# A four-layer graph network on one core: row sums of the adjacency moved to ScalarE, a lighter VectorE, and another order of the first steps

## The chip, the cores and the metric

One core of a Trainium2 chip runs the whole program. The metric is the device time of one execution in microseconds (us). The kernel before took 1369.27 us, the median of 3 runs (1369.18 to 1369.64). Measurements of this kernel tell a difference of about 0.2% (2.7 us) from none.

## The reference, cut to what matters

`x` is 4096x128, `adj` is 4096x4096, both float32. Four layers follow one another; each normalises its input, rectifies it, multiplies it by `adj`, and adds the layer's result to `x`:

```python
h = jnp.maximum(_layernorm(x, axis=-1), 0.0)
x = x + _L0_gnn_ref(h, adj, L0_gnn_W, L0_gnn_b)      # relu([h, adj @ h] @ W.T + b)
h = jnp.maximum(_layernorm(x, axis=-1), 0.0)
x = x + _L1_gnn_ref(h, adj, L1_gnn_W, L1_gnn_b)      # needs the row sums of adj
h = jnp.maximum(_layernorm(x, axis=-1), 0.0)
x = x + _L2_gnn_ref(h, adj, ...)                     # adj @ h, then a GRU cell
h = jnp.maximum(_layernorm(x, axis=-1), 0.0)
x = x + _L3_gnn_ref(h, adj, ...)                     # row sums, top 4 neighbours of every row by distance, adj again
```

Layers 1 and 3 scale by the inverse root of the row sums of `adj` (layer 1 with 1 added), so the sums of all 4096 rows have to be known before layer 1's operand is ready.

## The kernel before, in words

**Tiling.** The rows are cut into 8 row blocks of 512 (`NB`, `BLK`). A pass over `adj` multiplies each of the 8 row blocks with 8 column blocks. The unit of work is a *visit*: 2 tiles of 128 columns by 512 rows of the transposed `adj` (`at_in`, 512 KB), so that a row block of a pass has 16 visits (`UNITS`). Each visit's unit is loaded by SP into one of 10 slots of `ring` (L391), and the load of visit n waits until TensorE has used visit n-10 (`used`) and, in the first pass, until VectorE has summed it (`summed`). Layers 0 to 3 are passes 0 to 3, a fourth sparse-plus-dense product (pass 4) ends the program, and between passes 3 and 4 lies a search for the 4 nearest rows.

**Two ways to multiply.** A *whole* visit feeds the float32 tile directly (L469, two matmuls, which the trace shows as 4 records). A *split* visit has ScalarE round the unit to `A_hi` (`upper`, L803 to L810, recorded at L679), VectorE subtract to get `A_lo` (`lower`, L1111), and TensorE run three faster matmuls per tile (L464 to L466). Passes 1 to 3 split every visit. In pass 0 a visit is split if it serves two layers at once (a *shared* visit, `feeds` of two) or if the planner thinks VectorE has time. Six `A_hi` slots (`STAGED`) let ScalarE run up to six split visits ahead of TensorE.

**The plan.** Class `Plan` (L74) walks the visits with an estimated clock `self.us` (1.38 us for a split feed, 1.73 us for a whole one) and a second one for VectorE, `self.vector_us`. In pass 0 it adds 1.22 us for each unit that VectorE adds up and, if the clock leaves room, splits the visit and adds another 1.22 us (L172 to L174). It also places the small steps of each finished row block (`CHAIN`, L41) after certain visits, in the order in which each engine issues them; an engine never goes past a step that waits.

**Row sums.** `add_unit` (L985) adds every unit of pass 0 to `colsum` on VectorE, `fold` (L999) closes a row block, `degree_sums` (L548) lets TensorE sum over the partitions, and `degrees` (L1010) copies the result out; `degree_roots` (L743) follows on ScalarE. Then `residual`, `roots` and `normalise` on VectorE and ScalarE, `h_transposes` (L505) on TensorE, `rectify` (L717) on ScalarE, and `operand` (L530) on TensorE make the next layer's operand of this row block.

**The start.** For each row block b of `x` VectorE takes `statistics` (L949) and `normalise` (L958), TensorE transposes the result (`first_transposes`, L511), ScalarE rectifies it (`first_rectify`, L838), TensorE multiplies by the neighbour weight (`first_operand`, L520), and ScalarE copies that out to `G_first` (`first_operand_out`, L842). TensorE does the transposes of row blocks 0 and 1, then the product of row block 0, then the first visit (L611 to L615); the rest of the row blocks follow every second visit. ScalarE's loop over b is at L849.

Of the kernel before, what the change touches and what calls it, by code (L numbers as in the profile page):

```python
# [5 lines left out]
P = 128  # L6
N = 4096
BLK = 512
TPB = BLK // P
# [29 lines left out]
VECTOR_US, VECTOR_ROWS_US, BEHIND_US = 1.22, 6.0, 0.0  # L39
LEAD = {"PE": 0, "ACT": 4, "DVE": 3}  # L40
# [33 lines left out]
class Plan:  # L74
# [29 lines left out]


# [47 lines left out]

    def next_of(self, p, b, left):
# [7 lines left out]
    def visit(self, p, b, kb, left, may_share):  # L162
# [65 lines left out]
def gnn_stack(nc, x_in, at_in, pack_in, scaled_rows, out):  # L228
# [4 lines left out]
    with ctx:  # L233
# [47 lines left out]
        sq_aug = at("sq_aug", [P, NB, BLK], r32, sums_at)  # L281
        gate_r, new, gate_z, cand = (colsum[:, i, :] for i in range(4))
# [8 lines left out]
        rstd = sb("rstd", [P, TPB])  # L291
        degree = sb("degree", [P, NB, TPB])
        deg_pair = sb("deg_pair", [P, 2, TPB])
# [32 lines left out]
        used, summed = sem("used"), sem("summed")  # L326
# [3 lines left out]
        nat_full = sem("nat_full")  # L330
        stats_ready, std_ready, hn_ready = sem("stats_ready"), sem("std_ready"), sem("hn_ready")
# [30 lines left out]
        row_end = lambda p, b: PLAN.spans[p, b, p][1] + 1  # L362
        slot_of = lambda v: PLAN.split_count[v.n] % STAGED
# [17 lines left out]
        def _(sp):  # L381
# [3 lines left out]
            def load_unit(v):  # L385
                s = v.n % SLOTS
                if v.n >= SLOTS:
                    sp.wait_ge(used, v.n - SLOTS + 1)
                    if v.n - SLOTS < NB * UNITS:
                        sp.wait_ge(summed, v.n - SLOTS + 1)  # L390
# [23 lines left out]
        def _(pe):  # L414
# [262 lines left out]
        def _(act):  # L677
# [133 lines left out]

            def step(name, p, b):
# [24 lines left out]

            def first_rectify(b):  # L838
# [106 lines left out]
        def _(dve):  # L945
# [39 lines left out]
            def add_unit(v):  # L985

                s, j = v.n % SLOTS, v.n % UNITS
# [6 lines left out]
                else:  # L994
                    dve.wait_ge(summed, v.n - 1)
# [3 lines left out]
            def fold(b):  # L999

                dve.wait_ge(summed, UNITS * (b + 1))
# [8 lines left out]
            def degrees(b):  # L1010
# [3 lines left out]
                v_.tensor_copy(degree[:, b, :], ps[:, AUX, 0:TPB])  # L1014
                v_.tensor_copy(deg_pair[:, 0, :], ps[:, AUX, 0:TPB])
# [328 lines left out]
```

## Time and profile before

| what | value |
|---|---|
| median of 3 runs | 1369.27 us |
| the profiled execution | 1368.41 us |
| its span, first to last instruction | 1366.5 us |
| TensorE busy | 1313.5 us (96%) |
| VectorE busy | 1129.6 us (83%) |
| ScalarE busy | 795.4 us (58%) |
| GpSimd busy | 134.2 us (10%) |
| bytes moved | 291.49 MB, mean 213 GB/s |
| granted TensorE clock, mean | 0.996 |

The busy times are averages over stages with different limits. Matmul records overlap, so the time of a visit is read from starts, not from durations. Pass 0 lies between 14 us and 323 us; passes 1 to 3 reach to about 900 us, the search to about 1156 us, the last pass to the end.

### The profile page before, as it was taken

The numbers are of one execution on the slowest core, as the hardware profiler recorded it, in microseconds if no ns is written. First come the engines' busy times: TensorE is split into PE (matmuls) and PEld (weight loads), VectorE is DVE, ScalarE is ACT, GpSimd is POOL, SyncE is SP. The second block draws the span as 40 slices with busy tenths as digits, with TensorE's granted clock in tenths as the row PEclk, the third lists the DMA queues.
The fourth block names the chain that finished last, engine by engine and source line by source line (L and its number), as shares of the span: only waits on it lengthen the run. The fifth ranks groups of instructions, "written<-read, shape, count | busy, mean of one in ns | idle before, by whom it ended". The sixth has DMA issues, their size and how long they took to land.

```text
span 1366.5 us, 15557 instructions
## 1 busy us (share of the span) xinstructions
PE 1313.5 (96%) x5452; PEld 960.5 (70%) x5452; DVE 1129.6 (83%) x1538; ACT 795.4 (58%) x1173; POOL 134.2 (10%) x146
## 2 busy tenths in 40 slices
PE   7999999999899999999999999998999999999997
PEld 4556677778777875778777777876677777656664
DVE  8998889988999797767664898769999999845665
ACT  2322233446666587766555678655666565568885
POOL 0000000000000000000000100000000000077775
PEclk9999999999999999999999999999999999999999
DMA  9777766557876695566555889910111111499996
GB/s 354 232 261 243 233 203 209 190 185 244 298 265 227 192 352 170 192 225 204 190 186 172 306 285 321 350 58 1 39 54 54 54 39 54 156 354 385 383 383 231
DMA packets 82862, 291.49 MB, mean 213 GB/s; under 512 B 10849, under 2 KB 10977, under 8 KB 82785
## 3 DMA queue, kind: packets, MB, share of 16 engines
q1 hardware_dynamic: 78048, 280.01, 59.5%
q0 software_dynamic: 4736, 10.49, 2.3%
q8 instruction: 44, 0.72, 0.2%
q14 instruction: 34, 0.27, 0.1%
HBM read 286.27 MB, written 4.19 MB: 213 GB/s over the span
## 4 chain that ended last, share of the span: by engine, by line
PE 66%; DVE 29%; ACT 2%; issue 2%; DMA 0%; SPq 0%; ACTq 0%; DVEq 0%
PE ps L469 15%; PE ps L464 14%; PE ps L466 14%; PE ps L465 13%; DVE best_at L1187 9%; DVE rows_T L1183 9%; DVE A_lo L1111 5%; PE ps L539 1%; PE ps L567 1%; PE ps L568 1%; PE ps L502 1%; PE ps L508 1%; DVE hn L966 1%; PE ps L526 1%; DVE stats L951 1%
## 5 line engine op out<-in xcount | busy, mean ns | idle before, releaser
L679 ACT ACTIVATE A_hi<-ring 128x1024 fp32r<-128x1024 f32 x378 | 390.3, 1055 | 104.5 <-PE ps L466 91.9
L1111 DVE TENSOR_TENSOR A_lo<-ring,A_hi 128x1024 fp32r<-128x1024 f32 x333 | 395.7, 1218 | 55.3 <-ACT A_hi L679 53.0
L464 PE MATMUL ps<-A_hi,G_odd_hi 128*128 128x512 f32 x602 | 256.2, 426 | 2.1 <-DVE A_lo L1111 2.1
L466 PE MATMUL ps<-A_hi,G_odd_lo 128*128 128x512 f32 x602 | 235.9, 392 | 0.0
L465 PE MATMUL ps<-A_lo,G_odd_hi 128*128 128x512 f32 x602 | 234.8, 390 | 0.0
L679 ACT ACTIVATE scores<-ps,neg_sq 128x1024 f32<-128x1024 f32 x128 | 137.4, 1112 | 51.6 <-PE ps L640 33.8
L464 PE MATMUL ps<-A_hi,G_even_hi 128*128 128x512 f32 x386 | 162.7, 421 | 0.2 <-DVE A_lo L1111 0.2
L469 PE MATMUL ps<-ring,G_last 128*128 128x512 f32 x332 | 152.5, 592 | 0.0
L466 PE MATMUL ps<-A_hi,G_even_lo 128*128 128x512 f32 x386 | 150.7, 391 | 0.0
L465 PE MATMUL ps<-A_lo,G_even_hi 128*128 128x512 f32 x386 | 150.3, 389 | 0.0
L1183 DVE MAX8 rows_T<-scores 128x8 f32<-128x4096 f32 x32 | 141.3, 4415 | 7.3 <-ACT scores L679 7.3
L1187 DVE FIND_INDEX8 best_at<-rows_T,scores 128x8 uint32<-128x4096 f32 x32 | 141.4, 4419 | 0.0
L464 PEld LDWEIGHTS ps<-A_hi,G_odd_hi 128*128 128x128 f32 x602 | 113.5, 188 | 34.3 <-issue 13.0
L465 PEld LDWEIGHTS ps<-A_lo,G_odd_hi 128*128 128x128 f32 x602 | 113.6, 189 | 30.5 <-issue 9.6
L996 DVE TENSOR_TENSOR colsum<-colsum,ring 128x1024 f32<-128x1024 f32 x112 | 133.6, 1218 | 0.0
L466 PEld LDWEIGHTS ps<-A_hi,G_odd_lo 128*128 128x128 f32 x602 | 113.2, 188 | 24.9
L1305 POOL DMA_INDIRECT landing<-scaled_rows,best_at x128 | 123.7, 967 | 43.9 <-issue 36.0
L637 PE MATMUL ps<-sq_aug,ones 128*128 128x512 f32 x256 | 108.8, 425 | 14.8 <-ACT scores L679 14.1
L469 PE MATMUL ps<-ring,G_first 128*128 128x512 f32 x252 | 113.3, 592 | 0.0
L640 PE MATMUL ps<-z_hi,z_lo 128*128 128x512 f32 x256 | 101.7, 397 | 0.0
L638 PE MATMUL ps<-z_hi 128*128 128x512 f32 x256 | 101.5, 396 | 0.0
L469 PEld LDWEIGHTS ps<-ring,G_last 128*128 128x128 f32 x332 | 62.7, 189 | 55.0 <-issue 49.9
(136 smaller groups left out, 1516.1 us busy)
## 6 DMA issues: line engine op xcount, KB each, us to landing
ring<-adj_t SPq DMA_DIRECT2D x524, 512.0 KB, 4.8
X<-x_rows SPq DMA_DIRECT2D x8, 256.0 KB, 7.0
scaled_rows<-G_last POOLq DMA_DIRECT2D x8, 256.0 KB, 2.7
landing<-scaled_rows,best_at POOLq DMA_INDIRECT x128, 5.4
out_rows<-X SPq DMA_DIRECT2D x8, 256.0 KB, 5.7
pack<-packed SPq DMA_DIRECT2D x1, 836.0 KB, 14.7
pack<-packed SPq DMA_DIRECT2D x1, 192.0 KB, 3.5
```

The source lines that it names most:

```text
L464: mm(acc, G_hi[odd][:, kb, t, :], hi, start=start, stop=False)
L465: mm(acc, G_hi[odd][:, kb, t, :], lo, start=False, stop=False)
L466: done = mm(acc, G_lo[odd][:, kb, t, :], hi, start=False, stop=stop)
L469: done = mm(acc, G[:, kb, t, :], ring[:, s, k, :], start=start, stop=stop)
L637: mm(ps[:, bank, :], ones2[:, :], sq_aug[:, c, :], start=True, stop=False)
L640: last = mm(ps[:, bank, :], lo, z_hi[:, c, :], start=False, stop=True)
L679: return nc.scalar.activation(out_ap, in_ap, func, **k)
L996: ins = v_.tensor_tensor(half, half, ring[:, s, :, :], ALU.add)
L1111: v_.tensor_tensor(A_lo[:, s, :, :], ring[:, s, :, :], hi, ALU.subtract).then_inc(lower_ready, 1)
L1183: own.add(v_.max(best[:, seek[i], :], scores[i % 2][:, :]))
L1187: v_.max_index(best_at[:, seek[i], :], best[:, seek[i], :], scores[i % 2][:, :]).then_inc(scanned, 1)
L1305: pool.indirect_dma_start(out=landing[:, k, r, :], out_offset=None, in_=scaled_rows, in_offset=bass.IndirectOffsetOnAxis(ap=best_at[:, t, ...
```

## The change

1. TensorE's start: after the transposes of row block 0 comes its weight product (`first_operand(0)`), then the first visit; the transposes of row block 1 stand behind the first visit, the product of row block 1 and the transposes of row block 2 behind the second.
2. From row block 1 on ScalarE normalises `x` (`first_normalise`): VectorE makes a scale and a shift per row (`first_scales`), ScalarE applies them in four activations per row block, between `first_rectify(b)` and `first_operand_out(b)`.
3. A second copy of `adj`, in row order, is passed in (`rows_in`). Quarters of 1024 columns of some row blocks (`ROW_PIECES`) are no longer added up on VectorE: one quarter of row blocks 2 and 6, two quarters of 3, 4 and 5. Instead GpSimd loads 32 pieces of 128x1024 (512 KB each) into two buffers, the load of piece i after piece i-2 is summed, and ScalarE adds each up with the accumulator of a copy (`add_piece`). That takes 32 of 128 `add_unit` calls away. `degrees` adds the parts.
4. The planner's VectorE clock no longer counts the missing units. With the same rule it splits 21 more visits of pass 0: 3 in row block 2, 5 in row block 3, 6 in row block 4, 4 in row block 5 and 3 in row block 6. All other visits, their order and the plan from visit 112 on are the same; a few steps of row blocks 1 to 5 stand one visit later.
5. SP's loads wait for `summed` only where VectorE adds the unit.

```diff
+PIECE = 1024
+ROW_PIECES = ((), (), (2,), (2, 3), (2, 3), (2, 3), (3,), ())
...
+    def by_columns(self, b, u):
+        return u * UK * P // PIECE not in ROW_PIECES[b]
...
-                self.vector_us = max(self.vector_us, self.us - 4 * VECTOR_US) + VECTOR_US
+                self.vector_us = max(self.vector_us, self.us - 4 * VECTOR_US)
+                self.vector_us += self.by_columns(b, kb * HALVES + half) * VECTOR_US
                 split = split or b > 0 and self.vector_us + VECTOR_US <= self.us + SPLIT_US + BEHIND_US
...
             first_transposes(0)
-            first_transposes(1)
             first_operand(0)
             for v in PLAN.visits[:UNITS]:
                 visit(v)
-                if v.u % HALVES == 0 and v.u // HALVES + 1 < NB:
+                if v.u == 0:
+                    first_transposes(1)
+                elif v.u == 1:
+                    first_operand(1)
+                    first_transposes(2)
+                elif v.u % HALVES == 0 and v.u // HALVES + 1 < NB:
...
+            def add_piece(b, n, c):
+
+                i = pieces.index((b, n, c))
+                act.wait_ge(row_loaded[i % 2], 16 * (i // 2 + 1))
+                f(row_piece[:, i % 2, :], row_piece[:, i % 2, :], ACT.Copy,
+                  accum_out=row_sum[:, b, n, c:c + 1]).then_inc(row_summed, 1)
...
+            def first_normalise(b):
+                act.wait_ge(scale_ready, b)
+                if b >= 2:
+                    act.wait_ge(hT_full, b - 1)
+                for n in range(TPB):
+                    last = f(first_hn[b % 2][:, n, :], X[:, b, n, :], ACT.Identity,
+                             scale=first_scale[:, b % 2, n:n + 1], bias=first_shift[:, b % 2, n:n + 1])
+                last.then_inc(hn_ready, 1)
...
                 first_rectify(b)
+                if b + 1 < NB:
+                    first_normalise(b + 1)
                 first_operand_out(b)
...
                 if v.split:
                     upper(v)
+                if v.n in PLAN.row_sums:
+                    add_piece(*PLAN.row_sums[v.n])
                 for name, p, b in PLAN.due["ACT"].get(v.n, ()):
...
-                v_.tensor_copy(degree[:, b, :], ps[:, AUX, 0:TPB])
-                v_.tensor_copy(deg_pair[:, 0, :], ps[:, AUX, 0:TPB])
-                v_.tensor_scalar(deg_pair[:, 1, :], ps[:, AUX, 0:TPB], 1.0, None, ALU.add).then_inc(pair_ready, 1)
+                if not ROW_PIECES[b]:
+                    own.add(v_.tensor_copy(degree[:, b, :], ps[:, AUX, 0:TPB]))
+                else:
+                    dve.wait_ge(row_summed, 1 + max(i for i in range(len(pieces)) if pieces[i][0] == b))
+                    own.add(v_.tensor_tensor(degree[:, b, :], row_sum[:, b, :, 0], ps[:, AUX, 0:TPB], ALU.add))
...
+            for i, (b, n, c) in enumerate(pieces):
+                if i < 2:
+                    pool.wait_ge(used, b * UNITS - SLOTS)
+                else:
+                    pool.wait_ge(row_summed, i - 1)
+                pool.dma_start(row_piece[:, i % 2, :], rows_in[b, n, ROW_PIECES[b][c], :, :]).then_inc(row_loaded[i % 2], 16)
```

**TensorE at the start of the program.** `hn` and `nat` hold the normalised rows of even and odd row blocks, `in_a` the rectified ones. Before:

```order
L516 MATMUL ps<-pack,hn 128x128 x4
L516 MATMUL ps<-pack,nat 128x128 x4
L526 MATMUL ps<-pack,in_a 128x128 x4
L430 MATMUL ps<-in_a,pack 128x512
L469 MATMUL ps<-ring,G_first 128x512 x2
L516 MATMUL ps<-pack,hn 128x128 x4
L526 MATMUL ps<-pack,in_a 128x128 x4
```

With the change:

```order
L542 MATMUL ps<-pack,hn 128x128 x4
L552 MATMUL ps<-pack,in_a 128x128 x4
L456 MATMUL ps<-in_a,pack 128x512
L495 MATMUL ps<-ring,G_first 128x512 x2
L542 MATMUL ps<-pack,nat 128x128 x4
L495 MATMUL ps<-ring,G_first 128x512 x2
L552 MATMUL ps<-pack,in_a 128x128 x4
L542 MATMUL ps<-pack,hn 128x128 x4
L495 MATMUL ps<-ring,G_first 128x512 x2
```

The four transposes of row block 1 have moved from the second place to behind the first visit, and the third visit now stands directly behind the product of row block 1 and the transposes of row block 2.

**ScalarE at the seam between row blocks 2 and 3.** `rows_T` is row block 2's result being moved out, `deg_root`, `std` and `hTs` are `degree_roots`, `roots` and `rectify` of row block 2, `A_hi` is one split visit, `row_piece` one piece of row sums. Before:

```order
L679 ACTIVATE rows_T<-ps,pack 128x512 [waits nat_full,used]
L679 ACTIVATE A_hi_65<-ring_58 128x1024 [waits used,at_loaded3]
L679 ACTIVATE deg_root<-deg_pair 128x8 [waits pair_ready]
L679 ACTIVATE std<-meanvar,eps_ln 128x4 [waits stats_ready]
L679 ACTIVATE A_hi_65<-ring_58 128x1024 [waits used,at_loaded6]
L679 ACTIVATE hTs<-ps 128x512 [waits g_full,hT_full]
```

With the change:

```order
L709 ACTIVATE rows_T<-ps,pack 128x512 [waits nat_full,used]
L709 ACTIVATE A_hi_65<-ring_58 128x1024 [waits used,at_loaded3]
L709 ACTIVATE row_piece_68,row_sum<-row_piece_68 128x1024 [waits row_loaded0]
L709 ACTIVATE deg_root<-deg_pair 128x8 [waits pair_ready]
L709 ACTIVATE A_hi_65<-ring_58 128x1024 [waits used,at_loaded4]
L709 ACTIVATE std<-meanvar,eps_ln 128x4 [waits stats_ready]
L709 ACTIVATE A_hi_65<-ring_58 128x1024 [waits used,at_loaded5]
L709 ACTIVATE row_piece_68,row_sum<-row_piece_68 128x1024 [waits row_loaded1]
L709 ACTIVATE A_hi_65<-ring_58 128x1024 [waits used,at_loaded6]
L709 ACTIVATE A_hi_65<-ring_58 128x1024 [waits used,at_loaded7]
L709 ACTIVATE row_piece_68,row_sum<-row_piece_68 128x1024 [waits row_loaded0]
L709 ACTIVATE hTs<-ps 128x512 [waits g_full,hT_full]
```

Between `std` and `hTs` there was one `A_hi`; now there are three and two pieces.

## Rows read from the trace of the kernel before

**Rows 1.** The chain that ended last, by engine.

```profile
PE 66%; DVE 29%; ACT 2%; issue 2%; DMA 0%; SPq 0%; ACTq 0%; DVEq 0%
```

**Rows 2.** Waits of TensorE, 14 to 330 us: engine, line, cause: total us, times, longest.

```profile
PE ps L508 <- DVE hn L966: 1.1, 1, 1.1
PE ps L539 <- ACT hTs L679: 0.7, 1, 0.7
```

**Rows 3.** Chain in order of time (start, us, what) and TensorE's timeline, by visits.

```profile
22.27 3.44 PE ps L469 x8
27.04 3.44 PE ps L469 x8
...
88.00 6.87 PE ps L469 x16
```

**Rows 4.** TensorE's timeline inside row block 7, one feed apart.

```profile
299.90 0.39 PE L464 MATMUL ps<-A_hi,G_odd_hi 128*128 128x512 f32 x1
...
301.26 0.39 PE L464 MATMUL ps<-A_hi,G_even_hi 128*128 128x512 f32 x1
```

**Rows 5.** Timeline of the start: start, us, engine, line, operation, [idle before].

```profile
6.68 1.08 PE L516 MATMUL ps<-pack,hn 128*128 128x128 f32 x4 [6.68 <-DVE hn L966]
...
7.96 0.58 ACT L679 ACTIVATE in_a<-ps 128x512 f32<-128x512 f32 x1
...
10.68 1.12 PE L516 MATMUL ps<-pack,nat 128*128 128x128 f32 x4 [2.92 <-DVE nat L966]
...
11.59 1.92 PE L526 MATMUL ps<-pack,in_a 128*128 128x128 f32 x8
...
14.26 1.91 PE L469 MATMUL ps<-ring,G_first 128*128 128x512 f32 x4
```

**Rows 6.** Groups of ScalarE and VectorE instructions by form: xcount, busy us, mean ns.

```profile
L679 ACT ACTIVATE A_hi<-ring 128x1024 fp32r<-128x1024 f32 x378 | 390.3, 1055 | 104.5 <-PE ps L466 91.9 <-DMA ring<-adj_t 11.5
L1111 DVE TENSOR_TENSOR A_lo<-ring,A_hi 128x1024 fp32r<-128x1024 f32 x333 | 395.7, 1218 | 55.3 <-ACT A_hi L679 53.0
L679 ACT ACTIVATE in_a<-ps 128x512 f32<-128x512 f32 x24 | 14.3, 594 | 87.8 <-PE ps L466 78.9 <-PE ps L508 8.8
L679 ACT ACTIVATE rows_T<-ps,pack 128x512 f32<-128x512 f32 x8 | 5.5, 683 | 0.5 <-PE ps L469 0.5
L679 ACT ACTIVATION_READ_ACCUMULATOR hn<-nat 128x1 f32 x32 | 6.1, 190 | 0.0
```

**Rows 7.** Timeline at the seam of row blocks 2 and 3, three engines.

```profile
118.28 1.02 PE L430 MATMUL ps<-in_a,pack 128*128 128x512 f32 x2
...
129.01 0.60 PE L508 MATMUL ps<-pack,hn 128*128 128x128 f32 x4
...
119.55 1.06 ACT L679 ACTIVATE A_hi<-ring 128x1024 fp32r<-128x1024 f32 x1
...
126.42 0.30 ACT L679 ACTIVATE std<-meanvar,eps_ln 128x4 f32<-128x4 f32 x1 [4.04 <-DVE meanvar L955]
...
131.92 1.14 ACT L679 ACTIVATE G_odd_hi<-ps,inv_root 128x128 fp32r<-128x128 f32 x4 [1.68 <-PE ps L539]
...
126.97 1.12 DVE L966 TENSOR_SCALAR hn<-X,meanvar,rstd 128x128 f32<-128x128 f32 x4
```

**Rows 8.** Stretches (us), busy us (records) of each engine, granted clock, DMA share, GB/s.

```profile
118.28:154.62 36.34, 36.34 (x143) 24.79 (x142) 32.41 (x49) 10.99 (x17) 0.00 (x0) 1.00 0.71 232
154.62:193.30 38.68, 38.68 (x157) 27.41 (x156) 34.23 (x50) 12.17 (x18) 0.00 (x0) 1.00 0.68 217
1230.00:1330.00 100.00, 100.00 (x333) 60.98 (x333) 63.32 (x102) 86.45 (x147) 75.93 (x80) 1.00 1.02 383
```

**Rows 9.** Loads into `ring`, 1160 to 1366 us: issue to landing.

```profile
DMA to landing us min/median/max: 3.4/6.0/7.1
```

**Rows 10.** GpSimd's gathers: durations ns min/median/max, first and last start.

```profile
L1305 POOL DMA_INDIRECT landing<-scaled_rows,best_at x128: 940/944/1411, 1194.8 to 1356.3; - x128
```

**Rows 11.** Waits of VectorE, 60 to 330 us.

```profile
DVE A_lo L1111 <- ACT A_hi L679: 6.1, 4, 2.5
```

More of the change, by code:

```diff
@@ L102, in __init__ @@
         self.place(0.0, flush=True)
+        self.sum_count, self.row_sums, n = {}, {}, 0
+        for v in self.visits[:NB * UNITS]:
+            self.sum_count[v.n], n = n, n + self.by_columns(v.b, v.u)
+        self.sum_count[NB * UNITS] = n
+        for b in range(NB):
+            parts = [(b, n, c) for n in range(TPB) for c in range(len(ROW_PIECES[b]))]
+            for i, part in enumerate(parts):
+                self.row_sums[b * UNITS + (2 * i + 1) * UNITS // (2 * len(parts))] = part
         ended = [b * HALVES + half for b in sorted(range(NB), key=lambda b: self.rank[3, b]) for half in range(HALVES)]
@@ L325, in gnn_stack @@
         at_loaded = [sem(f"at_loaded{s}") for s in range(SLOTS)]
-        used, summed = sem("used"), sem("summed")
+        used, summed, row_summed = sem("used"), sem("summed"), sem("row_summed")
+        row_loaded = [sem(f"row_loaded{i}") for i in range(2)]
         upper_ready, lower_ready = sem("upper_ready"), sem("lower_ready")
@@ L362, in gnn_stack @@
         row_end = lambda p, b: PLAN.spans[p, b, p][1] + 1
+        pieces = [(b, n, c) for b in range(NB) for n in range(TPB) for c in range(len(ROW_PIECES[b]))]
         slot_of = lambda v: PLAN.split_count[v.n] % STAGED
@@ L388, in load_unit @@
                     sp.wait_ge(used, v.n - SLOTS + 1)
-                    if v.n - SLOTS < NB * UNITS:
-                        sp.wait_ge(summed, v.n - SLOTS + 1)
+                    before = PLAN.visits[v.n - SLOTS]
+                    if before.n < NB * UNITS and PLAN.by_columns(before.b, before.u):
+                        sp.wait_ge(summed, PLAN.sum_count[before.n] + 1)
                 sp.dma_start(ring[:, s, :, :], at_in[v.b, v.u, :, :, :]).then_inc(at_loaded[s], 16)
@@ L994, in add_unit @@
                 else:
-                    dve.wait_ge(summed, v.n - 1)
+                    dve.wait_ge(summed, n - 1)
                     ins = v_.tensor_tensor(half, half, ring[:, s, :, :], ALU.add)
@@ L1138, in step, with first_scales, first_statistics @@
                     square_parts(b)
+            def first_scales(b):
+                dve.wait_ge(std_ready, b + 1)
+                if b >= 3:
+                    dve.wait_ge(hn_ready, b - 1)
+                own.add(v_.reciprocal(first_scale[:, b % 2, :], std[:, b % 2, :]))
+                own.settle()
+                v_.scalar_tensor_tensor(first_shift[:, b % 2, :], meanvar[:, b % 2, :, 0], -1.0, first_scale[:, b % 2, :],
+                                        ALU.mult, ALU.mult).then_inc(scale_ready, 1)
+            def first_statistics(b):
+                dve.wait_ge(x_loaded[b], 16)
+                statistics(b, b, b % 2)
             def first_rows(b):
                 if b + 1 < NB:
-                    dve.wait_ge(x_loaded[b + 1], 16)
-                    statistics(b + 1, b + 1, (b + 1) % 2)
-                normalise(b, b, b % 2, first_hn[b % 2], 2)
-            dve.wait_ge(x_loaded[0], 16)
-            statistics(0, 0)
+                    first_statistics(b + 1)
+                first_scales(b)
+            first_statistics(0)
             normalise(0, 0, 0, first_hn[0], 2)
-            dve.wait_ge(x_loaded[1], 16)
-            statistics(1, 1, 1)
-            first_rows(1)
+            first_statistics(1)
+            first_scales(1)
+            first_statistics(2)
             for v in PLAN.visits[:UNITS]:
@@ L1168, in _ @@
             for v in PLAN.visits[UNITS:PLAN.rows_end]:
-                if v.feeds[0] == 0:
+                if v.feeds[0] == 0 and PLAN.by_columns(v.b, v.u):
                     add_unit(v)
@@ L1324 @@
     at = np.ascontiguousarray(get("adj").reshape(NB, BLK, UNITS, UK, P).transpose(0, 2, 4, 3, 1))
+    rows = np.ascontiguousarray(get("adj").reshape(NB, TPB, P, N // PIECE, PIECE).transpose(0, 1, 3, 2, 4))
     w0, w1, wm = get("L0_gnn_W"), get("L1_gnn_W"), get("L2_gnn_W_msg")
```

20 lines of the change are left out of this document (16 added, 4 removed).

## The prediction

> **What bounds the kernel now.** I read the chain of waits first: TensorE holds 66% of it and VectorE 29% [rows 1]. In order of time TensorE holds it from 14 us to 323 us, the whole of pass 0; VectorE takes over in passes 1 and 2 and in the search. The change touches pass 0 and the start only, so I then read who TensorE waits for there: two waits in 316 us, 1.1 us for `normalise` of row block 0 and 0.7 us for a `rectify` [rows 2]. Pass 0 is TensorE's own work and little else: what makes its work shorter makes the program shorter, and every new wait costs its full length.
>
> What a visit costs is read from starts. Sixteen records of whole visits, four visits, hold the chain for 6.87 us [rows 3]: 1.72 us each. The six matmuls of a split feed start 301.26 - 299.90 = 1.36 us apart from the next six [rows 4]. A split visit that serves one layer is 0.36 us cheaper on TensorE, if ScalarE and VectorE have prepared it in time.
>
> **The sum, edit by edit.**
>
> *More split visits.* 21 visits of pass 0 change from whole to split: 21 x 0.36 = **-7.5 us**. It is the main term.
>
> Their cover: each needs one `A_hi` on ScalarE (1.055 us) and one `A_lo` on VectorE (1.22 us) [rows 6]. VectorE gives up 32 `add_unit` calls and takes 21 subtractions of the same size, 11 fewer over the pass, about 13 us of work. In row block 4, the tightest, it goes from 9 + 16 = 25 such instructions to 15 + 8 = 23 while TensorE's time falls by 6 x 0.36 = 2.2 us. From 34.2 us busy in 38.7 us [rows 8] it comes to 31.8 in 36.5. VectorE stays ahead: cost nothing, and if it were behind, the rival on pass 1 below says what that costs.
>
> *Rows of `adj` summed on ScalarE.* One piece is like an `A_hi` plus the reading of the accumulator, 190 ns that partly overlap [rows 6]: between 1.06 and 1.25, I take 1.15 us. Eight pieces and five more `A_hi` bring row block 3 from 11.0 us busy [rows 8] to 25.5 us in a stage of 34.5. The mean is harmless; the order is not. ScalarE's waits are where the steps stand, and everything queues behind them. I follow the seam of row blocks 2 and 3, counting from 118.28 [rows 7].
>
> TensorE: `h_transposes` started at +10.7; two of the four visits between the seam's steps and it become split, so now at +10.0. One split visit and 0.35 us of transposes later, at +11.7, it wants `operand`, which needs `rectify`. ScalarE: `A_hi` starts at +1.3 [rows 7] and ends at +2.3, piece +3.5, `degree_roots` +4.3 (VectorE's sums are ready at about +4.1), `A_hi` +5.3. `std` stood at +8.1, after one `add_unit` that has gone, so it comes about 1 us sooner and ends at +7.5. Then three `A_hi` and two pieces, 3 x 1.05 + 2 x 1.15 = 5.4 us: +12.9. `rectify` takes 0.6 [rows 6]: +13.5. TensorE waits **+1.8 us**, once. `hn` itself was ready at +9.8 [rows 7] for +10.7 and is ready at +8.9 for +10.0.
>
> The same count at the seam after row block 3 (steps one visit later, so only two `A_hi` and one piece lie between) gives +11.9 for a need at +12.5: nothing. After row blocks 4 and 5 a sum and a subtraction now stand ahead of `normalise`, which ends at about +10.5 for a need at +10.7: I put **+0.3 us** for both. After row block 5 `operand` moves one visit behind `h_transposes`, with which it shared a visit; that takes out the 0.7 us wait of [rows 2]: **-0.7 us**. `degrees` grows by up to two tiny instructions with waits between, about 0.3 us, inside these margins; the 1.1 us wait of row block 0 stays.
>
> *The loads.* A unit or a piece is 0.524 MB; at the highest rate of the trace, 383 GB/s with the DMA engines full [rows 8], that is 1.37 us. Row block 3 moves 16 + 8 = 24 of them: 32.9 us in a stage of 34.5; row block 4 the same in 36.5. It fits, with 5% to spare, and ten slots of `ring` smooth it: no cost. The Trainium skill (DMA: Bandwidth & Descriptors, "Where 436 GB/s comes from") puts what HBM gives one core at about 358 GB/s. By that rule row block 3 would need 35.1 us and lose up to 0.6 us; the trace's 383 stands against it here.
>
> A piece's landing has to be quick too, for ScalarE waits for it in order. Two buffers mean that piece i is asked for when i-2 is summed, four visits ahead: at least 5.4 us in split visits of one feed, 10.9 in shared ones. Loads in the fullest stretch land after 3.4 to 7.1 us, median 6.0 [rows 9], and a GpSimd issue takes 0.94 us [rows 10]. So early in row blocks 3 to 5 a piece may be 1 to 2 us late, against ScalarE's lead of up to six split visits. I put nothing.
>
> *The start.* `rectify` of row block 0 ends at 7.96 + 0.58 = 8.54 [rows 5]. The weight product waited for the second transposes and began at 11.59; from there to the first visit, at 14.26, were 2.67 us, partly at half pace: four transposes take 1.08 us at 6.68 and 1.12 at 10.68 [rows 5], but 0.60 at 129.01 [rows 7]. Now it begins at about 8.6. At the old pace the first visit starts at 11.3; all at half pace nearer 12.1. I take 11.7: 2.5 us earlier.
>
> From this goes what the new order costs. The transposes of row block 1 (0.35 us) now lie behind the first visit. ScalarE's normalising of a row block is four activations like 1.14 us for four of the same size [rows 7], plus a per-row operand more, 0.683 - 0.594 = 0.09 us each [rows 6]: 1.5 us. In the second row block it stands ahead of `first_operand_out`, so the third visit waits about 0.3 us; the transposes of row block 3 wait for rectify and normalise behind that, 0.7 us. Later the cycle of 4.77 us [rows 3] leaves ScalarE 3.44 us for 3.0 us of work between product and transposes: no wait. The start gives 2.5 - 0.35 - 0.3 - 0.7 = **-1.2 us**, bounds -2.2 and -0.3. The seven normalisings that VectorE is rid of lie beside TensorE and bring nothing, as the split operands at the end of row block 0 are gated by its last product.
>
> *After pass 0.* From visit 112 on all is the same. VectorE waits 6.1 us for `A_hi` in pass 0 [rows 11], mostly at its end: it carries no debt into pass 1, so pass 1 starts earlier by what pass 0 gained, and the rest slides.
>
> Sum: -7.5 + 1.8 + 0.3 - 0.7 - 1.2 = **-7.3 us**. The profiled execution took 1368.41 us, 1.9 us more than its span, and comes to 1361.1; the median of the runs shown is 0.86 us above it. Predicted: **1362.0 us**, 0.5% faster.
>
> **Rivals.**
>
> *No queue on ScalarE.* If `rectify` is in time at the seam (pieces nearer 1.06 us, the seam's steps earlier), the 1.8 and 0.3 us go: 1359.9 us. For it: everything hangs on a 1.8 us overhang of an order counted. Chance 0.17.
>
> *Pieces land late, a little.* If issue to landing is 8 us with contention, two pieces take 9.2 us against 5.4 us early in each of row blocks 3 to 5; four such pairs of buffers eat ScalarE's lead and leave about 1.5 us per block: 1366.5 us. For it: the DMA engines are 95% taken. Against: loads at 383 GB/s still land in 6.0 us. Chance 0.13.
>
> *Pass 1 swallows it.* If VectorE, not TensorE's end of pass 0, sets when pass 1 proceeds, or the added splits are not ready in time, the 7.5 us is gone: 1369.3 less 1.2 plus 1 is 1369 us. For it: VectorE holds the chain right behind 323 us. Against: the 6.1 us that it waits just before [rows 11]. Chance 0.09.
>
> *Slower: pieces starve ScalarE.* Eight pieces in a row block go through two buffers, so the block lasts at least 4 x (issue + landing + 1.15). In row block 3 that exceeds 34.5 us from 7.5 us on, in row block 4 from 8.0, in row block 5 from 8.7. At 9 us the blocks last 40.6 us, 6.1 + 4.1 + 1.4 = 11.6 us more, and the total is 1373.6 us; it decides above about 8.6 us. What could make it so is GpSimd's issue being held up beside a VectorE that is busy nine tenths of the time. Against: with VectorE at 63% [rows 8] the gathers took 944 ns, 1411 at most [rows 10], where the blocks need 2 us more on every piece. The Trainium skill (SBUF: State Buffer, "SBUF: two separate sides") says that a DMA issued from GpSimd cannot get its descriptors written while VectorE runs a fast float32 copy; by that rule the two `colsum` copies that open a row block would hold up a piece. Chance 0.06.
>
> **How the numbers follow.** Forecast 0.55 (own range 1360 to 1365), no queue 0.17, late pieces 0.13, pass 1 swallows it 0.09, starving 0.06. The range reaches down past the no-queue case with the better start (1359) and up past the late pieces to 1367.5; it leaves out the last two cases and the tails. Faster by over 0.2% is below 1366.5: 0.55 + 0.17 + half of 0.13 and little else, 0.8. Within 0.2%: 0.13. Slower: 0.07. About 0.2% is what measurement tells from nothing.
>
> **What would show it.** In the changed profile: the first visit at 11.7 us; L508's counterpart waiting about 1 us in row block 1 and `operand` waiting 1.8 us behind `rectify` in row block 3 and nowhere else; starts of `begin`'s product 33 us apart in row block 2, 36 in row block 3, 36.5 in row block 4; pieces of about 1.15 us with landings of 5 to 7 us; DMA share near full in row block 3. I am wrong if TensorE waits for `A_lo` in row blocks 3 to 5 (late pieces or ScalarE's queue), or if pass 0 ends 7 us earlier and the later stages do not.

## The result, and the profile after

The changed kernel takes 1361.59 us, the median of 5 runs (1361.28 to 1362.47), against 1369.27 (5 runs beside them): ratio 0.9938, 95% interval 0.9927 to 0.9949. The forecast was 1362.0. The profiled execution took 1361.59 us, with a span of 1359.8 us against 1366.5.

The chain and the waits of TensorE up to 330 us in the profile after, to be laid beside [rows 1, 2]:

```profile
PE 66%; DVE 30%; ACT 3%; issue 2%; DMA 0%; ACTq 0%; DVEq 0%
```

```profile
PE ps L534 <- DVE hn L1016: 1.2, 1, 1.2
PE ps L565 <- ACT hTs L709: 0.8, 1, 0.8
PE ps L542 <- ACT nat L709: 0.3, 1, 0.3
PE ps L495 <- ACT G_first L709: 0.2, 1, 0.2
```

The bound is what it was. The wait of 1.1 us for `hn` in row block 1 is still there (1.2). The 0.7 us wait for `hTs` has gone from row block 6 and one of 0.8 us has come in row block 3. The last two are new, at the start.

Where pass 0 is shortened can be read from where each row block starts: `begin`'s product, L430 before and L456 after, on TensorE. The timeline of the kernel after:

```profile
50.13 1.02 PE L456 MATMUL ps<-in_a,pack 128*128 128x512 f32 x2
...
83.53 1.02 PE L456 MATMUL ps<-in_a,pack 128*128 128x512 f32 x2
...
116.84 1.02 PE L456 MATMUL ps<-in_a,pack 128*128 128x512 f32 x2
...
152.53 1.02 PE L456 MATMUL ps<-in_a,pack 128*128 128x512 f32 x2
...
189.10 1.02 PE L456 MATMUL ps<-in_a,pack 128*128 128x512 f32 x2
...
228.37 1.02 PE L456 MATMUL ps<-in_a,pack 128*128 128x512 f32 x2
...
270.35 1.02 PE L456 MATMUL ps<-in_a,pack 128*128 128x512 f32 x2
...
316.78 0.95 PE L582 MATMUL ps<-ones,nat 128*128 128x1 f32 x8
```

| row block | starts before, us | starts after, us | lasts before | lasts after | splits added |
|---|---|---|---|---|---|
| 1 | 50.65 | 50.13 | 33.33 | 33.40 | 0 |
| 2 | 83.98 | 83.53 | 34.30 | 33.31 | 3 |
| 3 | 118.28 | 116.84 | 36.34 | 35.69 | 5 |
| 4 | 154.62 | 152.53 | 38.68 | 36.57 | 6 |
| 5 | 193.30 | 189.10 | 40.69 | 39.27 | 4 |
| 6 | 233.99 | 228.37 | 43.97 | 41.98 | 3 |
| 7 | 277.96 | 270.35 | 46.43 | 46.43 | 0 |

(Row block 7 is counted to the `degree_sums` that close it, 324.39 and 316.78 us.) Pass 0 ends 7.6 us earlier, of which 0.5 comes from before row block 1. The shift is 7.7 us still at the first `lap_rows` step of pass 3 (782.3 to 774.6 us), 6.9 us at the second (790.7 to 783.8) and when the search starts (902.0 to 895.1) and 6.7 us at the end of the span.

Stretches of row blocks 3 and 4 after, against [rows 8] (columns as there):

```profile
116.84:152.53 35.69, 34.84 (x153) 26.54 (x152) 29.26 (x44) 24.87 (x38) 3.70 (x7) 1.00 0.95 346
152.53:189.10 36.57, 36.57 (x170) 29.61 (x168) 32.92 (x49) 27.83 (x43) 4.88 (x9) 1.00 0.95 358
```

ScalarE goes from 11.0 to 24.9 us busy in row block 3 and from 12.2 to 27.8 in row block 4, the DMA share from 0.7 to 0.95. VectorE goes from 32.4 to 29.3 and from 34.2 to 32.9. TensorE stays busy but for 0.85 us. The pieces:

```profile
L1363 POOL DMA_DIRECT2D row_piece<-adj_rows x32: 528/528/963, 64.6 to 233.0; - x32
L709 ACT ACTIVATE row_piece<-row_piece x32: 1039/1057/1079, 69.3 to 252.5; 128x1024 f32<-128x1024 f32 x32
L709 ACT ACTIVATION_READ_ACCUMULATOR row_piece<-row_piece x32: 180/187/218, 70.2 to 253.5; 128x1 f32 x32
...
DMA to landing us min/median/max: 4.0/6.6/8.1
```

The issue costs 0.53 us (the gathers of [rows 10] take 0.94), the landing 6.6 us in the median. ScalarE waited for pieces 8 times, 11.8 us in all, and TensorE never noticed.

The seam of row blocks 2 and 3, ScalarE's timeline after (start, us, instruction):

```profile
118.11 1.06 ACT L709 ACTIVATE A_hi<-ring 128x1024 fp32r<-128x1024 f32 x1
119.05 1.06 ACT L709 ACTIVATE row_piece<-row_piece 128x1024 f32<-128x1024 f32 x1
...
123.98 0.30 ACT L709 ACTIVATE std<-meanvar,eps_ln 128x4 f32<-128x4 f32 x1 [1.96 <-DVE meanvar L1005]
124.19 1.04 ACT L709 ACTIVATE A_hi<-ring 128x1024 fp32r<-128x1024 f32 x1
125.14 1.05 ACT L709 ACTIVATE row_piece<-row_piece 128x1024 f32<-128x1024 f32 x1
...
126.17 1.99 ACT L709 ACTIVATE A_hi<-ring 128x1024 fp32r<-128x1024 f32 x2
128.07 1.04 ACT L709 ACTIVATE row_piece<-row_piece 128x1024 f32<-128x1024 f32 x1
...
129.11 0.57 ACT L709 ACTIVATE hTs<-ps 128x512 f32<-128x512 f32 x1
```

and what TensorE does with it:

```profile
129.74 1.16 PE L565 MATMUL ps<-pack,hTs 128*128 128x128 f32 x8 [0.85 <-ACT hTs L709]
```

`std` ends at +7.4 us from the row block's start, `hTs` at +12.8, the product starts at +12.9. TensorE was ready for it at +12.05 (0.85 us of waiting). It is the queue that the prediction counted, ending 0.7 us sooner than the +13.5 counted there.

### The profile page after: what moved, and what is told of

Its sections match the earlier page's. It is cut to its first block, busy times and chain, and to the rows that moved or that the text cites. A ratio compares the mean times of both kernels' runs of the same rounds, so it can differ in the third digit from the quotient of the medians.

```text
span 1359.8 us, 15719 instructions
## 1 busy us (share of the span) xinstructions
PE 1309.5 (96%) x5494; PEld 969.0 (71%) x5494; DVE 1112.4 (82%) x1509; ACT 861.1 (63%) x1286; POOL 151.5 (11%) x178
## 4 chain that ended last, share of the span: by engine, by line
PE 66%; DVE 30%; ACT 3%; issue 2%; DMA 0%; ACTq 0%; DVEq 0%
PE ps L490 14%; PE ps L492 14%; PE ps L491 14%; PE ps L495 12%; DVE best_at L1258 9%; DVE rows_T L1254 9%; DVE A_lo L1170 5%; PE ps L565 1%; PE ps L593 1%; PE ps L594 1%; PE ps L528 1%; DVE hn L1016 1%; DVE stats L1001 1%; PE ps L534 1%; PE ps L552 1%
## 5 line engine op out<-in xcount | busy, mean ns | idle before, releaser
L709 ACT ACTIVATE A_hi<-ring 128x1024 fp32r<-128x1024 f32 x399 | 412.6, 1055 | 113.1 <-PE ps L492 89.6
L1170 DVE TENSOR_TENSOR A_lo<-ring,A_hi 128x1024 fp32r<-128x1024 f32 x354 | 420.2, 1218 | 68.6 <-ACT A_hi L709 66.1
L490 PE MATMUL ps<-A_hi,G_even_hi 128*128 128x512 f32 x428 | 178.8, 418 | 0.2 <-DVE A_lo L1170 0.2
L492 PE MATMUL ps<-A_hi,G_even_lo 128*128 128x512 f32 x428 | 167.1, 390 | 0.0
L491 PE MATMUL ps<-A_lo,G_even_hi 128*128 128x512 f32 x428 | 166.7, 390 | 0.0
L667 PE MATMUL ps<-sq_aug,ones 128*128 128x512 f32 x256 | 108.6, 424 | 13.6 <-ACT scores L709 12.9
L669 PE MATMUL ps<-z_lo,z_hi 128*128 128x512 f32 x256 | 102.0, 398 | 0.0
L1047 DVE TENSOR_TENSOR colsum<-colsum,ring 128x1024 f32<-128x1024 f32 x80 | 95.8, 1217 | 0.0
```

Source lines behind the costliest of these rows:

```text
L490: mm(acc, G_hi[odd][:, kb, t, :], hi, start=start, stop=False)
L491: mm(acc, G_hi[odd][:, kb, t, :], lo, start=False, stop=False)
L492: done = mm(acc, G_lo[odd][:, kb, t, :], hi, start=False, stop=stop)
L667: mm(ps[:, bank, :], ones2[:, :], sq_aug[:, c, :], start=True, stop=False)
L669: mm(ps[:, bank, :], hi, z_lo[:, c, :], start=False, stop=False)
L709: return nc.scalar.activation(out_ap, in_ap, func, **k)
```

## The experiments

The theory that goes into them: the gain is 21 x 0.36 us of cheaper TensorE work, VectorE's relief is only what makes it possible, one wait behind the pieces takes some back, and the start brings little.

### Parts of the change alone

**The start's order alone**, on the kernel before:

```diff
             first_transposes(0)
-            first_transposes(1)
             first_operand(0)
             for v in PLAN.visits[:UNITS]:
                 visit(v)
-                if v.u % HALVES == 0 and v.u // HALVES + 1 < NB:
+                if v.u == 0:
+                    first_transposes(1)
+                elif v.u == 1:
+                    first_operand(1)
+                    first_transposes(2)
+                elif v.u % HALVES == 0 and v.u // HALVES + 1 < NB:
```

> The kernel before with TensorE's new order at the start and nothing else: VectorE still normalises all of x, no pieces, no added splits. My theory: the first visit starts about 2 us earlier (near 12.3 us), 0.35 us is lost to the transposes that now lie behind it, and VectorE, which is as busy as TensorE in the first row block (4.9 us of work per cycle of 4.77), gives back up to 0.7 us: 0.9 us faster than before, about 1368.4 us, and row block 1 starts near 49.8 us. Rival: VectorE's normalising cannot follow an earlier TensorE at all, so the start brings nothing (row block 1 at 50.6 us, 1369.3 us), and it is ScalarE's normalising that makes the start's gain possible.

Measured: 1368.72 us against 1370.21, ratio 0.9990 (0.9980 to 0.9999), so anything from 0.1 to 2.7 us faster. In its profile row block 1 starts at 50.66 us, where it did before. The first visit does start 2.2 us earlier, but look how long it takes (TensorE's timeline):

```profile
12.07 3.16 PE L469 MATMUL ps<-ring,G_first 128*128 128x512 f32 x4
...
15.07 0.60 PE L516 MATMUL ps<-pack,nat 128*128 128x128 f32 x4
```

3.0 us from its start to the next step, where the kernel before needs 1.76 (from 14.26 [rows 5] to this line) and a later visit 1.72:

```profile
16.02 0.60 PE L516 MATMUL ps<-pack,hn 128*128 128x128 f32 x4
```

TensorE did not wait in it: it worked at half pace for most of it. Neither theory had that. The rest of the row block has no wait but 0.2 us, so the rival (VectorE cannot follow) falls.

**No pieces**, start and ScalarE's normalising kept:

```diff
-ROW_PIECES = ((), (), (2,), (2, 3), (2, 3), (2, 3), (3,), ())
+ROW_PIECES = ((), (), (), (), (), (), (), ())
```

> The changed kernel without row pieces: all sums on VectorE and the split visits as in the kernel before; only the start (order, ScalarE normalises) is left. My theory: pass 0 runs as before behind a start that is 0.5 us earlier, row block 1 at 50.1 us, total 1368.8 us. Rival: the start is worth the 1.2 us of the forecast and more because VectorE is freer, and the pieces hide it: 1368 us or less.

Measured: 1369.44 us, ratio 0.9995 (0.9986 to 1.0005). Row block 1 starts at 49.88 us and every later row block lasts what it did before, to 0.1 us. Row block 1 starts 0.8 us earlier than in the profile before; the timed runs put the start's worth between 1.9 us gained and 0.7 lost.

**Pieces, but the old splits:**

```diff
-                self.vector_us += self.by_columns(b, kb * HALVES + half) * VECTOR_US
+                self.vector_us += VECTOR_US
```

> The changed kernel with its 32 pieces, but the planner counts VectorE's time as before, so that the 21 added split visits are whole again. My theory: relief of VectorE by itself is worth nothing, the 7.5 us come from the cheaper visits alone: pass 0 as in the kernel before, 1368.8 us, and no waits behind pieces, as ScalarE has more room. Rival: taking the sums away from VectorE is what shortens pass 0, and about half of the gain, 3 to 4 us, stays (1365 us).

Measured: 1369.53 us, ratio 0.9995 (0.9986 to 1.0005). Row blocks 2 to 7 last exactly as before (34.30, 36.34, 38.68 us and so on), with 32 pieces loaded and summed beside them. The relief goes into VectorE's idle time: between 60 and 330 us it now waits

```profile
DVE degree L1069 <- PE ps L582: 42.2, 5, 10.8
```

42.2 us for TensorE (18.9 before). Its `colsum` work between 60 and 330 us falls from 133.1 to 95.9 us. Taking 37 us of work from an engine that is 90% busy but not the bound is worth nothing. The rival falls.

**The added splits with all sums on VectorE**, old start (the planner gets `by_columns` and `ROW_PIECES` for its clock; `add_unit`, `degrees` and the loads stay as before):

> The kernel before with the 21 added split visits and all 128 sums still on VectorE (old start, no pieces). My theory: VectorE becomes the bound in row blocks 3 to 5: 29 to 31 instructions of 1.13 to 1.22 us and about 6 us of steps against 34.5 to 39 us of TensorE, about 39.5, 41 and 41 us per block; 5 + 4.5 + 2 us lost against 7.5 gained, so about 1373 us, slower than before by 4 us, with TensorE waiting for A_lo. Rival: VectorE's lead and idle time carry it, the splits bring their 7.5 us without any relief, 1362 us, and the pieces were not needed.

Measured: 1377.31 us, ratio 1.0053 (1.0036 to 1.0069): slower than before. Row blocks 3, 4 and 5 in its trace:

```profile
118.59:158.09 39.50, 36.09 (x153) 26.16 (x152) 38.89 (x54) 18.31 (x24) 0.00 (x0) 1.00 0.62 214
158.09:200.70 42.61, 38.22 (x170) 30.50 (x169) 42.09 (x58) 18.32 (x24) 0.00 (x0) 0.96 0.58 198
200.70:245.97 45.27, 42.32 (x181) 33.95 (x180) 44.75 (x60) 18.32 (x24) 0.00 (x0) 0.92 0.56 187
```

VectorE is busy 38.9 of 39.5, 42.1 of 42.6 and 44.8 of 45.3 us: it is the bound. In these three row blocks TensorE waits 8.8 us for `hn` and only 2.0 us for `A_lo`, which I had expected to be the wait. The size was off: row block 3 lasts what I counted, the next two 1.6 and 4.3 us more. Two things that my count per row block left out stand in the rows: VectorE has 54, 58 and 60 records there, work handed on from the row block before among them, and TensorE's granted clock is 0.96 and 0.92 in the last two. How much each adds was not separated. So the pieces are worth all that the splits cost otherwise: 1377.3 against 1361.6 us is what summing 32 units elsewhere does once the splits are there, but for the start, which is the old one here.

### The pieces: their place and their lateness

**The due steps ahead of the piece** in ScalarE's loop:

```diff
                 if v.split:
                     upper(v)
-                if v.n in PLAN.row_sums:
-                    add_piece(*PLAN.row_sums[v.n])
                 for name, p, b in PLAN.due["ACT"].get(v.n, ()):
                     step(name, p, b)
+                if v.n in PLAN.row_sums:
+                    add_piece(*PLAN.row_sums[v.n])
```

> The changed kernel with one edit: at every visit ScalarE first does the steps that are due and then adds up the piece. At the seam of row blocks 2 and 3 the rectify comes one piece (1.05 us) earlier. My theory: the 0.8 us wait of operand for hTs in row block 3 goes and nothing else changes: row block 3 lasts 34.8 instead of 35.7 us, 1360.7 us in all. Rival: the wait was set by hT_full or by the loads of the pieces, and the time stays at 1361.6.

Measured: 1361.38 us, ratio 0.9935 (0.9918 to 0.9953). In the total it can't be told from the change. In the trace it can: the wait for `hTs` is gone, row block 3 lasts 34.66 us instead of 35.69, the others the same. This kernel gives the worth of the splits without that wait, from the row blocks' lengths against before: 0.98 + 1.68 + 2.12 + 1.42 + 1.98 = 8.2 us, of which 0.7 is the wait that went from row block 6: 7.5 us for 21 splits.

**Later pieces.** Small memsets of 128x300, each waited for, stand ahead of each piece's load on GpSimd, 3 in the first kernel and 9 in the second:

```diff
+                for k in range(DELAYS):
+                    g.memset(delay[:, :], 0.0).then_inc(delayed, 1)
+                    pool.wait_ge(delayed, DELAYS * i + k + 1)
                 pool.dma_start(row_piece[:, i % 2, :], rows_in[b, n, ROW_PIECES[b][c], :, :]).then_inc(row_loaded[i % 2], 16)
```

> The changed kernel with every piece's load held back on GpSimd by three small memsets, each waited for, about 1.1 us. My theory (pieces through two buffers: a row block with 8 pieces lasts at least 4 x (issue + landing + sum), with the measured 0.53 + 6.6 and 1.2 us that is 33.3 us, close under TensorE's 34.8): with 1.1 us more it is 37.8 us, row block 3 grows by about 2 us and row block 4 by about 1 us less what ScalarE's lead covers: 1363 to 1365 us. Rival: ScalarE's lead covers it all, 1361.6 us.

Measured: 1364.91 us, ratio 0.9961 (0.9948 to 0.9974), inside the expected span. The three memsets held a load back by 1.47 us (126.58 to 128.05 us for one of them), more than the 1.1 counted. The profiled execution took 1369.13 us, the slowest of six (the others 1363.8 to 1365.6), so its row blocks show where the loss falls and overstate its size: row block 3 lasts 36.39 us (0.7 more than in the change) and row block 4 40.82 (4.3 more). TensorE waits for `hTs` once in each, 1.6 and 2.4 us. Most of what is left of the 4.3 us is slower work: behind the wait of 2.4 us, the granted clock is 0.50 between 170 and 172 us and 0.65 in the 2 us after.

> The same with nine memsets, about 3.2 us later per piece. My theory: row blocks 3, 4 and 5 last about 46 us each whatever TensorE does, 10 + 10 + 7 us more, less if landings get shorter as the queues thin out: 1380 to 1389 us, slower than before, with ScalarE waiting for row_piece and TensorE for A_lo. Rival: the waits hide in ScalarE's idle time and the time stays under 1366 us.

Measured: 1385.83 us, ratio 1.0103 (1.0072 to 1.0135). The nine memsets held a load back by 3.9 us (127.59 to 131.49), where 3.2 was counted. Its three row blocks with 8 pieces:

```profile
117.05:161.44 44.39, 37.71 (x154) 28.86 (x153) 30.85 (x45) 24.77 (x38) 28.37 (x78) 0.88 0.79 278
161.44:207.14 45.70, 40.34 (x170) 31.73 (x169) 33.06 (x49) 28.50 (x43) 32.94 (x87) 0.93 0.79 284
207.14:253.01 45.87, 42.32 (x181) 34.06 (x180) 33.90 (x51) 25.81 (x38) 29.27 (x76) 0.93 0.79 278
```

44.4, 45.7 and 45.9 us, near the 46 us that was expected, but that number was met partly by luck. Four round trips of a buffer, with what this run shows for each part, are 4 x (3.9 + 0.53 + 5.2 landing in the median + 1.03) = 42.6 us: the landings got shorter, as the expectation allowed. The 2 to 3 us above that were not taken apart; TensorE's granted clock is 0.88 to 0.93 in these blocks. ScalarE waits 20 times for a piece, and TensorE behind it, for `hTs`, `hn` and `rows_T` and not for `A_lo`, as I had expected:

```profile
ACT row_piece L711 <- DMA row_piece<-adj_rows: 53.2, 20, 5.9
```

```profile
PE ps L567 <- ACT hTs L711: 12.1, 3, 6.7
PE ps L536 <- DVE hn L1018: 2.8, 1, 2.8
PE ps L530 <- ACT rows_T L711: 0.7, 1, 0.7
```

That pieces can starve ScalarE and so hold up TensorE is shown. So the change stands near an edge: 1.5 us more on each piece costs about 3 us in the total, and 3.9 us more makes the whole slower than before.

**More of the same**: steps ahead of pieces, and a quarter of row block 1 as well:

```diff
-ROW_PIECES = ((), (), (2,), (2, 3), (2, 3), (2, 3), (3,), ())
+ROW_PIECES = ((), (2,), (2,), (2, 3), (2, 3), (2, 3), (3,), ())
```

> The kernel with the steps ahead of the pieces, and one quarter of row block 1 also summed on ScalarE (36 pieces); the planner then splits 3 more visits in row block 1 and 1 more in row block 3. My theory: 4 x 0.36 = 1.4 us less TensorE time, DMA at 20 units in 32.3 us in row block 1 fits: 1359.3 us if the wait of row block 3 is also gone. Rival: the loads are full in row blocks 2 and 3 by then and pieces come late, 1361 us or more.

Measured: 1359.97 us, ratio 0.9927 (0.9909 to 0.9945). Row block 1 lasts 32.67 us (0.73 less for 3 splits, 1.08 counted) and row block 3 34.20 (0.46 less than with the steps first, 0.36 counted); row block 4 gives 0.3 of that back, 36.87 us against 36.56. TensorE has no wait in it, and in the two kernels below with the same pieces it lasts 36.57, so the 0.3 is no price of the added pieces. In the total this kernel is not resolved from the change.

### The start

TensorE's timeline in the kernel after, up to its first visit, for [rows 5]:

```profile
6.84 1.09 PE L542 MATMUL ps<-pack,hn 128*128 128x128 f32 x4 [6.84 <-DVE hn L1016]
8.76 2.08 PE L552 MATMUL ps<-pack,in_a 128*128 128x128 f32 x8 [0.83 <-ACT in_a L709]
10.63 1.84 PE L456 MATMUL ps<-in_a,pack 128*128 128x512 f32 x2
12.31 1.88 PE L495 MATMUL ps<-ring,G_first 128*128 128x512 f32 x4
14.03 0.60 PE L542 MATMUL ps<-pack,nat 128*128 128x128 f32 x4
```

Product and L456 take 3.55 us to the first visit, 2.67 before. In the eight profiles of kernels with this start and no matmuls added ahead of it, the first visit begins at 12.05 to 12.45 us; it takes 1.72 us in three of them (this one among them) and 2.1 to 3.0 in five. To see whether the half pace is what holds the start, ten float32 matmuls of a constant tile keep TensorE busy before its first step:

```diff
-            pe.wait_ge(pack_loaded, 16)
             pe.wait_ge(consts_set, 1)
+            for _ in range(10):
+                mm(ps[:, first_G[1], 0:P], ones2[:, :].bitcast(fp32), ones2[:, :].bitcast(fp32), start=True, stop=True)
+            pe.wait_ge(pack_loaded, 16)
             first_transposes(0)
```

> The changed kernel with ten extra 128x128 float32 matmuls on TensorE (a constant tile times itself into a free bank, overwritten later) before the first transposes, from about 1.4 to 6.2 us. In the runs so far TensorE worked at half pace until somewhere between 11 and 14 us, and the first visit took 1.7 us when the pace rose before it and up to 3.0 us when not. My theory: that half pace, not the order of the steps, is what held the gain of the start at 0.5 us. With TensorE busy before, the first weight product takes 1.0 instead of 1.9 us, the first visit starts near 10.9 us and takes 1.72, row block 1 starts near 48.7 us, and the total falls by about 1.5 us to 1360.1. Rival: the start is held by ScalarE (normalise, then the copy of the product), so the first visit stays at 12.3 us and row block 1 at 50.1 us.

Measured: 1361.19 us, ratio 0.9938 (0.9921 to 0.9955): not to be told from the change in time. In its profile:

```profile
1.35 4.63 PE L637 MATMUL ps<-ones 128*128 128x128 f32 x20 [1.35 <-POOL eps_d L1357]
6.54 0.63 PE L542 MATMUL ps<-pack,hn 128*128 128x128 f32 x4 [0.56 <-DVE hn L1018]
8.45 1.16 PE L552 MATMUL ps<-pack,in_a 128*128 128x128 f32 x8 [1.29 <-ACT in_a L711]
9.45 1.02 PE L456 MATMUL ps<-in_a,pack 128*128 128x512 f32 x2
10.54 1.98 PE L495 MATMUL ps<-ring,G_first 128*128 128x512 f32 x4
```

The transposes take 0.63 instead of 1.09 us, the product 1.0 from start to start instead of 1.87, and row block 1 starts at 48.46 us, 1.7 us sooner. So the half pace was the limit in this execution. Its span is only 0.8 us shorter than the change's, though. The matmuls do not bring the full pace in every execution, as the next three show, and the four timed runs do not resolve it.

> The kernel before with the same ten matmuls. My theory: product and L430 at full pace save 1.3 us: first visit near 12.9 us instead of 14.3, row block 1 near 49.3 us, about 1368 us. With e10 this gives the worth of the new start at a like pace: about 0.6 us. Rival: the extra matmuls delay the first transposes and bring nothing.

Measured: 1369.69 us, ratio 1.0000 (0.9990 to 1.0009). The transposes of row block 0 ran at full pace (0.63 us), but then TensorE idled 3.1 us for VectorE, and everything from 10.33 us to the first visit, at 14.65, was at half pace again; row block 1 started at 51.27 us. The expectation failed, and with it the comparison at a like pace.

> The kernel with steps ahead of pieces and a quarter of row block 1 on ScalarE, with the ten matmuls. The gains add: 1.5 to 2 us under that kernel, 1358 us. Rival: the starts of that kernel's row blocks are gated elsewhere and nothing adds.

Measured: 1359.10 us, ratio 0.9913 (0.9896 to 0.9929). In the profiled execution the ten matmuls did nothing for the pace (transposes 1.09 us, first visit 2.8 us, row block 1 at 51.02 us). The gain over its twin without them, 0.9 us, is within the spread; the 1.5 to 2 us that were expected did not show.

> The same with VectorE normalising all of x as in the kernel before. In the run with the new order alone the stretch from the end of the first visit to row block 1 was 35.6 us against 36.1 with ScalarE normalising (two waits, 0.3 and 0.2 us). My theory: ScalarE's normalising costs about 0.3 us here, so this is as fast or up to 0.5 us faster, 1357.8 us. Rival: with TensorE earlier, VectorE, 95% busy in the first row block, falls behind and TensorE waits for hn and nat: 1 us or more slower than its twin.

Its edit puts VectorE's `normalise` back for all row blocks of `x` and takes `first_normalise` out. Measured: 1357.88 us, ratio 0.9911 (0.9894 to 0.9927), the fastest of all, though not resolved from its twin. The traces do resolve one thing: from the end of the first visit to row block 1 it takes 35.59 us here and in the kernel with the start's order alone, and 36.10 us wherever ScalarE normalises (no pieces, pieces with old splits, the change: 36.11, 36.10, 36.10). ScalarE's normalising of `x` costs 0.5 us. VectorE keeps up without it.

## Why the prediction was right

**The splits, -7.5.** Right: 7.5 us, read from the row blocks of the kernel with the steps first. The price of a split, 0.36 us from [rows 3, 4], held to a few hundredths. The argument that VectorE's relief is cover and not gain held from both sides: the relief alone gives nothing (1369.5 us), the splits alone lose 7 us (1377.3). The cover was thinner than counted: in row block 4 VectorE is busy 32.9 us, not 31.8, of 36.6.

**The wait at the seam of row blocks 2 and 3, +1.8.** The place, the cause and the only-once were right; it measured 1.0 us, 35.69 - 34.66. The main mis-sized term is the length of the queue, 5.4 us for three `A_hi` and two pieces: I added durations of 1.05 and 1.15, where instructions back to back overlap, 0.95 from start to start, and a piece with its readout takes 1.03. That makes 4.9 us. The rest is that TensorE wants the result later than the +11.7 I counted: without the wait, in the kernel with the steps first, its product starts at +11.9 (129.55 - 117.67).

**The tight seams, +0.3, and the merged step, -0.7.** The first measured nothing (row block 5 lasts 39.27, and 40.69 less 4 x 0.36 is 39.25). The second came as said: row block 6 is 1.99 us shorter, of which 1.08 are splits.

**The start, -1.2.** It gave -0.5 in the profiled execution, inside its bounds. The failed step is "all at half pace nearer 12.1, I take 11.7": the first visit began at 12.31, as TensorE's half pace covered the whole product and L456. The waits that the new order brings were 0.25 and 0.30 us, not 0.3 and 0.7. What I did not see at all is that the half pace can reach into the first visit too. Over the seven profiles with this start, ScalarE normalising and no extra matmuls, the change among them, row block 1 begins at 49.88 to 51.12 us, mean 50.5. The old start, too, depends on when the pace rises. It was profiled twice without extra matmuls, at 50.65 us in the kernel before and here in the one with all sums on VectorE, whose first row block is the same:

```profile
51.67 1.02 PE L436 MATMUL ps<-in_a,pack 128*128 128x512 f32 x2
```

So -0.5 us is one draw. Whether the start is worth nothing or about a microsecond stays open; that it fell inside the bounds is partly luck.

**After pass 0.** The rest slid, as [rows 11] let one expect: the 7.6 us hold up to pass 3. The rival on pass 1 falls. Between the first two `lap_rows` steps of pass 3, 0.8 us are lost. TensorE waits there for `in_b` as before (1.85 us, 1.82 before), but behind that wait its granted clock is 0.50 between 774 and 776 us in the profile after, and 1.00 at the same place in the one before. "The rest slides" had no term for that.

**The loads.** Row blocks 3 and 4 run at 346 and 358 GB/s with no stall on TensorE, as the 383 GB/s of [rows 8] allowed. But 383 was not the highest rate of the trace, as the prediction called it; between 14 and 20 us, with a share of 1.04 (1.02 there), the kernel before moves 409:

```profile
14.00:20.00 6.00, 6.00 (x24) 3.37 (x24) 5.54 (x21) 2.08 (x6) 0.00 (x0) 1.00 1.04 409
```

The Trainium skill's 358 GB/s (DMA: Bandwidth & Descriptors, "Where 436 GB/s comes from") is passed in both profiles, the one after moving 406 GB/s between 14 and 20 us. The change itself does not test the 35.1 us that row block 3 would need by that rule, as the block lasts 35.69 with its wait. The kernel with the steps first does: there row block 3 lasts 34.66 us, and row block 4 runs at 369 GB/s, neither with a wait of TensorE.

**Late pieces.** ScalarE did wait for pieces in row blocks 3 and 4, 7 times and 10.9 us, up to 3.5 us at once. Its lead took them up, as no wait of TensorE for `A_lo` stands in pass 0. That the prediction put nothing was right.

**The starving rival** is a real mechanism, as the later pieces show, and did not happen here: issue plus landing is 0.53 + 6.6 = 7.1 us, under the 7.5 from which row block 3 grows. GpSimd's issue takes 528 ns in the median and 963 at most. The long ones go with what the prediction named, a `colsum` copy on VectorE: the issue at 112.20 us takes 0.96 us beside the two copies from 112.35 to 113.65, and the one at 163.77 takes 0.64 beside the copy that starts at 163.61. The traces of the nine kernels with pieces have twelve issues longer than 0.6 us, besides the first piece's 0.72, and each of the twelve overlaps such a copy. The longest take 1.37 us, one in each of the three kernels with a quarter of row block 1 on ScalarE, and start with the copies (51.88 and 51.84 us in the first of them). Two more issues overlap a copy and take 0.53 all the same. So a copy can hold an issue up, by 0.1 to 0.8 us, where the blocks would have needed 2 us on every piece.

**The sum** in the profiled execution: -7.5 + 1.0 - 0.7 - 0.5 + 0.1 (row block 1) = -7.6 us at the end of pass 0, -7.3 predicted. Two errors of 0.7 and 0.8 us, in the start and at the seam, went opposite ways: the total is nearer than its terms, and that is luck. So is part of the last step to 1362.0. From profiled execution to profiled execution the gain is 6.8 us (1368.41 to 1361.59), half a microsecond less than the 7.3 predicted. The prediction then added 0.86 us, by which the profiled execution of before lay under its median, and the one after lies on its median. The two differences largely cancel in the 0.4 us by which the forecast missed.

## What to carry to other kernels

Relieve the engine that is not the bound only if the bound can spend the relief, and then look for the exchange rate: here 1.2 us of VectorE time bought a 0.36 us cheaper visit on TensorE, and either half alone is worth nothing or less. When work goes to an idle engine, count its queue from each step that somebody waits for, with start-to-start times, and put the steps ahead of the new work. A second stream through two buffers sets its own floor, uses / 2 x (issue + landing + use): know how far it is below the stage.

## What was not expected of the hardware

TensorE's pace at the start is not the granted clock of the rows, which stands at 1.00 there. The same four transposes take 1.09 us (half pace) or 0.60 to 0.63. The pace rose during the product or L430 in the kernel before, and in the new start without extra matmuls between about 12 and 15 us, by how long L456 and the first visit take, at a different point in each execution; a gain of 2 us in when TensorE starts was in part used up by working at half pace longer. Ten matmuls ahead brought the full pace in one execution of four for the whole start, for the first transposes alone in two, and not at all in one.

The granted clock itself falls from 1.00 (2.4 GHz) to 0.50 (1.2 GHz) in or right behind some waits of TensorE. In row block 3 of the kernel with the latest pieces TensorE waits 6.68 us for `hTs`, up to 135.8 us, and the clock is 0.50 from 133 to 141 us. In row block 5 of the one with all sums on VectorE it waits 2.95 us for `hn`, up to 214.5 us, and the clock is 0.50 from 214 to 220 us. A wait then costs more than its length. Behind the wait of 1.8 us in pass 3 the clock fell in the profile of the change and not in the one of before, so the length of that wait alone does not decide it.
